# A 28-turn attention and mixture-of-experts kernel on one core: router and layer norms moved to GpSimd, softmax inverse spread by TensorE, ScalarE's queue reordered

## Time and profile before

| | |
|---|---|
| median of three runs | 6423.66 us |
| the profiled execution | 6440.11 us, its span 6438.2 us |
| PE busy | 4737.3 us, 74% |
| DVE busy | 5596.4 us, 87% |
| ACT busy | 4054.4 us, 63% |
| POOL busy | 4425.8 us, 69% |
| mean granted TensorE clock | 0.730 |

### The profile page before, as it was taken

How to read it: one execution, slowest core, us unless ns; L and a number is a source line. 1 busy time by engine, 2 the same in 40 slices (tenths; PEclk the granted TensorE clock), 3 DMA queues, 4 the chain that set the end, 5 groups by cost and what they waited for, 6 DMA issues and landing times.

```text
span 6438.2 us, 135940 instructions
## 1 busy us (share of the span) xinstructions
PE 4737.3 (74%) x26938; PEld 2880.6 (45%) x26938; DVE 5596.4 (87%) x24453; ACT 4054.4 (63%) x10222; POOL 4425.8 (69%) x3986
## 2 busy tenths in 40 slices
PE   3566777777777777777777777777777777777776
PEld 1333444444444444444444444444444444444444
DVE  1999999988989998999989898989999899999941
ACT  2455666666666666666666666666666666666643
POOL 1667776767677776767677677767776777777742
PEclk9666767777777777777777777777777777777777
DMA  4111111111111111111111111111111111111100
GB/s 75 39 31 42 34 40 34 40 32 42 30 41 34 39 35 34 40 32 43 32 42 30 40 36 36 38 33 40 32 43 31 43 31 32 30 30 34 33 11 10
DMA packets 585501, 229.09 MB, mean 36 GB/s; under 512 B 481152, under 2 KB 580224, under 8 KB 584576
## 3 DMA queue, kind: packets, MB, share of 16 engines
q1 hardware_dynamic: 584576, 219.25, 15.4%
HBM read 150.14 MB, written 68.80 MB: 34 GB/s over the span
## 4 chain that ended last, share of the span: by engine, by line
PE 29%; ACT 18%; issue 16%; DVE 15%; POOL 12%; ACTq 0%; DVEq 0%; POOLq 0%; DMA 0%; SPq 0%
DVE b_v L452 7%; POOL b_r L502 5%; PE y_ps L685 4%; DVE b_r L463 4%; PE h_ps L611 4%; POOL c_h L762 4%; ACT b_x L478 3%; PE a_ps L666 3%; PE pT_ps L524 3%; PE o_ps L545 2%; ACT b_e L485 2%; ACT L737 2%; PE h_ps L666 2%; POOL b_rec L493 2%; ACT L478 2%
## 5 line engine op out<-in xcount | busy, mean ns | idle before, releaser
L463 DVE MATCH_REPLACE8 b_r<-b_v,b_r 128x256 f32<-128x256 f32 x4704 | 1879.1, 416 | 0.0
L502 POOL TENSOR_SCALAR b_r<-b_r,b_rec 128x256 f32<-128x256 f32 x1568 | 1777.1, 1147 | 119.6 <-POOL b_rec L493 119.6
L452 DVE MAX8 b_v<-b_r 128x8 f32<-128x256 f32 x4704 | 1649.2, 418 | 0.0
L524 PE MATMUL pT_ps<-k_ident,b_e 128*128 128x128 f32 x3136 | 669.9, 352 | 776.3 <-ACT b_pT L532 688.3
L493 POOL TENSOR_TENSOR b_rec<-b_den,k_mone 128x4 f32<-128x4 f32 x392 | 400.5, 1022 | 1153.5 <-ACT b_x L478 1150.2
L762 POOL TENSOR_TENSOR c_h<-c_h,c_cb 128x448 f32<-128x448 f32 x672 | 760.9, 1133 | 503.9 <-ACT c_cb L739 503.0
L524 PEld LDWEIGHTS pT_ps<-k_ident,b_e 128*128 128x128 f32 x3136 | 472.6, 180 | 1161.2 <-issue 1136.2
L510 POOL TENSOR_TENSOR b_e<-b_e,b_r 128x1024 f32<-128x1024 f32 x392 | 923.5, 2356 | 18.0 <-POOL b_r L502 14.4
L685 PE MATMUL y_ps<-k_w,c_h 128*112 128x64 f32 x5376 | 776.1, 298 | 181.1 <-POOL c_h L762 177.9
L685 PEld LDWEIGHTS y_ps<-k_w,c_h 128*112 128x112 f32 x5376 | 706.5, 210 | 404.1 <-issue 403.0
L452 DVE MAX8 b_v<-b_s 128x8 f32<-128x256 f32 x1568 | 551.1, 415 | 318.0 <-POOL b_e L510 201.2
(11 more groups left out here) (146 smaller groups left out, 7904.9 us busy)
## 6 DMA issues: line engine op xcount, KB each, us to landing
q_d<-a_qe SPq DMA_DIRECT2D x56, 448.0 KB, 4.2
b_k<-k_d SPq DMA_DIRECT2D x1568, 16.0 KB, 2.0
b_v<-v_d SPq DMA_DIRECT2D x1568, 16.0 KB, 2.0
b_q<-q_d SPq DMA_DIRECT2D x392, 64.0 KB, 2.1
c_win<-vpad_d SPq DMA_DIRECT2D x56, 145.0 KB, 2.8
c_hm<-cpad_d SPq DMA_DIRECT2D x56, 145.0 KB, 2.3
vpad_d<-a_vT SPq DMA_DIRECT2D x56, 116.0 KB, 3.7
c_win<-vpad_d SPq DMA_DIRECT2D x56, 116.0 KB, 2.7
```

The source lines that it names most:

```text
L452: top = dve.max(out=b_v8[p][:, t, 8 * rnd:8 * rnd + 8], in_=src[:, t, :])
L463: last = dve.match_replace(out=b_r[p][:, t, :], in_to_replace=b_v8[p][:, t, 8 * rnd:8 * rnd + 8], in_values=src[:, t, :], imm_value=GONE)
L502: last = pool.tensor_scalar(out=b_r[p][:, t, :], in0=b_r[p][:, t, :], scalar1=GONE, scalar2=b_rec[p][:, t:t + 1], op0=ALU.is_le, op1=ALU.mult)
L524: last = pe.transpose(pT_ps[:, col:col + 128], b_e[p][:, t, c * 128:(c + 1) * 128], k["ident"][:, :])
```

## The change

- Layer norms and the residual add of c0 and c1 go from VectorE to GpSimd (steps ADD and 1). VectorE keeps the means and variances.
- The router: VectorE now does only 4 MAX8 on the raw logits and 4 MATCH_REPLACE8 that overwrite the best two of 8 (buffer `lr`, with GONE in 6 more columns of it). ScalarE takes the exponentials of both copies; GpSimd subtracts one from the other and makes the weights by 10 small instructions (step 4).
- The inverse of the softmax sum: VectorE's reciprocal of region r-1, put into round 0 of region r, between the 4 MAX8 and the 4 replaces. The mask becomes one GpSimd instruction `b_r <= GONE` without the factor. TensorE spreads the inverse over 16 rows by 4 products with the identity into further columns of `o_ps`; ScalarE's copy of the values takes 256 columns in place of 128, and GpSimd multiplies once per strip (step NORM).
- ScalarE's queue in slot r becomes [0 to 0.2], turn(r-1) both halves, [0.2 to 0.6], values(r-1), [0.6 to 1], sum(r), exp(r), scores(r+2). The queues of TensorE and GpSimd keep their order.
- Some places move: c0's exponential of the router from 83.7 to 84.3 and c1's from 108.68 to 108.3 on ScalarE, c1's turn of the tokens and router product one slot earlier, c0's first product from 78.1 to 78.3.

```diff
-        def pool_inverse(pool, tau, r):
-            pool.wait_ge(b_sum, reg + 1)
-            pool.tensor_tensor(out=b_rec[p][:, :], in0=b_den[p][:, :], in1=k["mone"][:, 0:HP], op=ALU.pow).then_inc(b_inv, 1)
+        def dve_inverse(dve, tau, r):
+            reg = tau * SLOTS + r
+            dve.wait_ge(b_sum, reg + 1)
+            alone(dve)
+            dve.reciprocal(b_rec[r % RING][:, :], b_den[r % 2][:, :]).then_inc(b_inv, 1)
...
+                if rnd == 0 and older is not None:
+                    dve_inverse(dve, tau, older)
...
-            for t in range(HP):
-                last = pool.tensor_scalar(out=b_r[p][:, t, :], in0=b_r[p][:, t, :], scalar1=GONE, scalar2=b_rec[p][:, t:t + 1],
-                                          op0=ALU.is_le, op1=ALU.mult)
+            pool.tensor_scalar(out=b_r[p][:, :, :], in0=b_r[p][:, :, :], scalar1=GONE, scalar2=None,
+                               op0=ALU.is_le).then_inc(b_msk, 1)
...
+            pe.wait_ge(b_inv, reg + 1)
+            for t in range(HP):
+                pe.matmul(o_ps[32 * t:32 * t + VH, 128:256], b_rec[r % RING][:, t:t + 1].broadcast_to([128, VH]), k["ident"][:, :],
+                          start=True, stop=True)
...
                         before = on and (r >= 1 or not first)
-                        if on:
-                            act_sum(act, b, r)
-                            act_exp(act, b, r)
                         steps(act, "act", n, lo, r, fs, 0, 0.2)
                         if before:
                             act_turn(act, b, r - 1, 0)
-                        if on and (r + 2 < SLOTS or not last):
-                            act_scores(act, b, r + 2)
-                        if before:
                             act_turn(act, b, r - 1, 1)
                         steps(act, "act", n, lo, r, fs, 0.2, 0.4)
                         steps(act, "act", n, lo, r, fs, 0.4, 0.6)
                         if before:
                             act_values(act, b, r - 1)
                         steps(act, "act", n, lo, r, fs, 0.6, 1)
+                        if on:
+                            act_sum(act, b, r)
+                            act_exp(act, b, r)
+                            if r + 2 < SLOTS or not last:
+                                act_scores(act, b, r + 2)
...
+            if step == NORM:
+                pool.wait_ge(b_att, NWIN * (s + 1) + 1)
+                pool.tensor_tensor(out=b_at[i][:, 0:2], in0=b_at[i][:, 0:2], in1=b_at[i][:, 2:4], op=ALU.mult).then_inc(b_nrm, 1)
...
+            if step == 3:
+                pool.wait_ge(S["top"], s + 1)
+                pool.tensor_tensor(out=D["l"][:, :, :, :], in0=D["lr"][:, :, :, 0:NE],
+                                   in1=D["pv"][:, :, 6:7].unsqueeze(1).broadcast_to([TILE, 2, NT, NE]), op=ALU.subtract).then_inc(S["ls"], 1)
```

## The result

The changed kernel takes 9021.12 us (median of 4 runs, 9020.11 to 9021.82), the kernel before beside it 6426.64: a ratio of 1.404, 95% interval [1.401, 1.406]. The forecast was 8670 us, range 7800 to 9350: slower, by the mechanism named, 4% under the measured time.

What follows compares the result with a forecast made beforehand. A once-per-slot loop across the engines was to set the pace: 159 ahead, 660 for three turns, 6140 for twenty, 1440 for five, 276 and 15 behind, sum 8690; less 16 to the median, 8670 us, range 7800 to 9350.

Steps and rivals of the forecast that it cites:

- The step that carried it: ScalarE's sum(r) waits behind values(r-1), VectorE's next region behind sum(r): a loop once per slot, 307 us a turn against 222.5.
- the short loop alone: Rival: only exponentials, probabilities, transposes, values, sum count, about 11 us plus what is queued between; 7150 us, chance 0.08.
- The mask: GpSimd's single compare after the region's end: no row had it, bounds 1.1 and 4.5 us, taken as 1.4.
- slow mask: Rival: the compare made the old mask slow, so it stays at 4.5 us; a turn 337, 9400 us, chance 0.10.
- Class 2: Expert slot: reciprocal, region, mask, product, DOWN, values' copy, sum in series; 18.7 us.
- Class 0: Slot with c0's router exponential between two GELUs, c1's transposes and stage a, put behind the mask; 27.2 us.
- Class 3: Slot with c1's router exponential between two GELUs, waiting for GpSimd's subtraction behind mask and product; 23.1 us.
- Classes 1, 4 and 6: Slot without experts 25.0 us; slot with GpSimd's norm and router mix in series 15.8; slot with third group's product 21.2.
- The first three turns: Turns in which c0 and c1 fill up: 181 us, then some 237 and 242, 660 in all.
- the long loop: Per slot: sum(r-1), reciprocal, rest of region r, mask(r), product, DOWN, values(r-1), copy, sum(r); seven classes make 153.7 us.
- The rival in which VectorE keeps the pace: ScalarE returns before each region's last MAX8, the reciprocal never waits, 19 us a turn come off: 5890 us, chance 0.05.
- The drain of a table load: Skill's 1.38 us per switch of set on ScalarE; would add 12 us per seven slots, some 9300 us; prediction rejected it.

Runs made afterwards that it cites:

- both links open: Changed kernel with GpSimd's mask moved behind its steps of 0.2 to 0.5 and VectorE's reciprocal behind the region's last replace: 8145.47 us, ratio 1.267.
- old queue, late reciprocal: Changed kernel with ScalarE's queue order of before and the reciprocal of region r-1 behind the last replace of region r: 6466.02 us, ratio 1.005.
- the second mask instruction: Changed kernel with a second GpSimd mask instruction of the same size added behind the first: 9883.71 us, ratio 1.535.
- the fastest kernel: Changed kernel with ScalarE's queue order of before, reciprocal behind the region, router's exponentials back at 83.7 and 108.68: 6328.07 us, ratio 0.984.
- the kernel with ScalarE's old queue: Changed kernel with only ScalarE's order undone: sum(r), exp(r), then turn(r-1), scores, steps, values(r-1): 6519.37 us, ratio 1.012.

## Why the prediction was right, and where its sizes were off

The step that carried it, that sum(r) stands behind values(r-1) and VectorE's next region behind sum(r), is shown from three sides: undone at ScalarE it takes back 2502 of 2594 us, and opened at GpSimd or at VectorE it gives 0.8 to 0.9 ms, not more with both. What the prediction had wrong is the weight. It gave two thirds of the loss to this loop (8670 us against 7150 for the short loop alone); measured it is one third (9021 against 8145, 876 us), and the larger part is what the same queue order costs without it. By classes, first exponential to first exponential in full turns:

| class | 0 | 1 | 2 | 3 | 4 | 5 | 6 | sum |
|---|---|---|---|---|---|---|---|---|
| before | 14.7 | 19.0 | 19.1 | 12.0 | 13.1 | 16.6 | 16.3 | 110.9 |
| forecast | 27.2 | 25.0 | 18.7 | 23.1 | 15.8 | 22.7 | 21.2 | 153.7 |
| after | 30.3 | 23.3 | 21.8 | 24.0 | 15.3 | 23.4 | 20.7 | 158.7 |
| both links open | 30.6 | 23.3 | 17.1 | 18.9 | 15.3 | 17.9 | 19.7 | 142.8 |
| old queue, late reciprocal | 14.6 | 23.2 | 17.6 | 13.0 | 16.1 | 12.3 | 14.7 | 111.5 |

- The mask: forecast 1.4, taken near the cast. The profiled one takes 2.77 us, in the middle of the bounds 1.1 and 4.5. The rival "slow mask" was thus half right, and the 1.0 us that the prediction set beside it for one-input work isn't borne out. It is the largest mis-sized single term.
- Class 2 was 3.1 short: mask 1.4, the residual add of c0 0.7, which by its place 79.25 stands in front of the product and which I had left out there, and from the product's end to the start of the values' copy 3.4 where I had 2.5 (4132.64 to 4136.05). DOWN took 1.73 before the values could start, against 1.64 in the earlier trace rows, and the four new products 0.4; I had put these inside the old 2.4 without a term of their own.
- Class 0 was 3.1 short as well, and here it is the path that was wrong. I had it by the mask; the rows under the second mask instruction show another way of about the same length, and class 0 stays at 30.6 with both links open. Between the last two lines of the table, which differ in ScalarE's queue and in the place of the mask, lie 31 us, and 16 of them are in this class. Which steps of it make the 3.1 wasn't worked out.
- Class 3 came out near by luck, because two errors cancel: the mask 1.4 too small, and the table load that I put behind the wait lies within it.
- Classes 1, 4 and 6 were under the forecast, by 1.7, 0.5 and 0.5. I take these for overlaps that I had laid in series; no row was read for it.
- VectorE: 5010.8 us busy, forecast about 5050. Table loads 737 in place of 533 (without the first of either program), forecast some 200 more:

```profile
L741 ACT ACT_TABLE_LOAD x369 | 473.4, 1283 | 129.9 <-PE a_ps L670 43.3 <-PE h_ps L670 42.5 <-issue 38.3
L487 ACT ACT_TABLE_LOAD x260 | 333.6, 1283 | 4.6
L732 ACT ACT_TABLE_LOAD x108 | 138.6, 1283 | 2.0
```

- The first three turns took 198, 255 and 271 us against 181, 237 and 242, for the same reason as the classes: 64 us. Twenty full turns at 317.3 against 307: 206 us. The last five 301 against 288: 63 us. With 4 us less at the two ends these make up the 330 us between 8690 and the span of 9018.
- The short loop alone was priced at 7150 us, some 247 a turn; with both links opened it measured 8145, 285.6 a turn. In classes 2, 3, 5 and 6 this stayed out of the result, because the long loop is longer still there. I take the reason to be that I had counted what is queued between at its busy time, without the waits on TensorE inside it; this wasn't tested.
- The rival in which VectorE keeps the pace gave 5890. It fails even with the old queue (6466): I had read 201.5 of 222 us busy as the bound. VectorE's idle time in the earlier trace rows, both times for GpSimd's probabilities, was a sign that the rest of the turn belonged to the other queues.
- The drain of a table load, which the Trainium skill (ScalarE: Activation LUTs, What ACT_TABLE_LOAD costs) adds, isn't seen here either: in the lines above of class 3 the GELU's load starts 0.01 us after the exponential has ended and the GELU 0.02 us after the load, and in the slot of class 2 there are 2.74 us from the negated maximum's start to the exponentials of 256, which hold 0.2, one load of 1.28 and the sums of 1.24.

## What to carry to other kernels

Buffers in two copies let engines run a slot apart only while no queue asks for something of the same slot. When an item is moved in an in-order queue, follow what now stands ahead of it across all engines until the way ends or closes; if it closes, the pace is the sum around it, whatever the busy shares say. And when one ring is opened, look for the next: here the first was worth a third of the loss. An engine busy for nine tenths of a turn need not set it: with some 20 us a turn cut from VectorE and ScalarE's old order the kernel was no faster than before, and 1.6% faster once the router's exponentials were back in their old places in ScalarE's queue.

## What the runs showed of the hardware

- GpSimd: one compare of 128 x 1024 with an immediate takes 2.77 us (2767 to 2778 ns over 392), four of 128 x 256 with the second operation and a scalar from memory took 4.51. That is 2.7 ns an element against 1.8 of the cast and 2.3 of the two-input product over 1024 elements (2.35 us).
- A table load isn't held by the wait of the activation that needs it: in the slot above it ran at 4148.38, 4.4 us of idle time ahead of its exponential at 4154.04.
- TensorE's mean granted clock was 0.730 before, 0.639 after, 0.774 in the fastest kernel. In the changed kernel's class 2 the windows around DOWN show it at 0.50, the lower of the two levels (1.2 GHz), and DOWN took 1.73 us. The clock had fallen before that, between 4116 and 4120, after 4 us in which TensorE was busy 2.63 us. In class 0 of the same turn DOWN took 0.97 us in a window granted 1.00:

```profile
4112.00:4116.00 4.00, 2.63 (x40) 1.61 (x33) 0.00 (x0) 2.15 (x6) 0.00 (x0) 1.00 0.02 4
4116.00:4120.00 4.00, 2.21 (x3) 0.65 (x3) 2.46 (x12) 3.94 (x15) 0.92 (x1) 0.56 0.11 25
...
4132.00:4135.00 3.00, 2.19 (x20) 2.01 (x24) 0.00 (x0) 0.00 (x0) 1.75 (x2) 0.50 0.00 0
...
4216.00:4220.00 4.00, 3.36 (x42) 2.44 (x42) 0.00 (x0) 1.53 (x5) 1.58 (x2) 1.00 0.00 0
```

```profile
4216.64 0.97 PE L689 MATMUL y_ps<-k_w,c_h 128*112 128x64 f32 x8 [2.16 <-POOL c_h L813]
```

So a part of the loss can be the lower clock and not the waits themselves. How large it can be is estimated from the kernel with ScalarE's old queue, which has the same products. Its window of 226 us, a little over a turn:

```profile
3004.00:3230.00 226.00, 169.43 (x1109) 105.86 (x1101) 179.52 (x814) 159.60 (x381) 145.50 (x146) 0.75 0.16 36
```

TensorE is busy 169.4 us in it, and 196.8 in a turn of the changed kernel. That is 27 us more, where the turns of the two kernels differ by 93. How much of the 27 lies on the ring was not separated.
